# Flamingo block, attention stage: first queries, key stacks, zero rows and a weights' part in another order

## What is computed

```python
x = x + tanh(g_xattn[0]) * attention(layernorm(x), ctx_2048, ctx_2048, gamma)
x = x + tanh(g_ffn[0]) * ffn(layernorm(x), ...)

def attention(q, k, v, gamma):            # 16 x 128 x 512 each, 8 heads
    qk = einsum('bhdq,bhdl->bhql', qh, kh) / sqrt(16)
    return gamma * einsum('bhql,bhdl->bhdq', softmax(qk), vh)

def ffn(x):                               # per token, top 2 of 8 experts
    h = x @ down_w + down_b
    # sum over the two chosen experts e: gate * (gelu(gelu(h) @ w1[e] + b1[e]) @ w2[e] + b2[e])
    # plus 0.1 * the shared expert, then up_w, up_b, and gelu(x) @ core_w + core_b
```

## Time and profile before

| | us |
|---|---|
| median of 3 runs | 739.79 |
| lowest and highest run | 738.60, 742.24 |
| the profiled execution | 746.0 |
| its span | 744.2 |
| first matmul | 15.94 |
| TensorE busy | 688.2 (92%) |
| ScalarE, VectorE, GpSimd busy | 538.1, 532.0, 485.9 |

### The profile page before, as it was taken

One profiled execution on the slowest core, in us unless ns is written; L12 is line 12 of the kernel. 1 busy time (PEld: TensorE's weight loads), 2 busy tenths in 40 slices (PEclk: granted clock), 3 DMA queues, 4 the chain that ended last, 5 costly groups with the idle time before them and its releaser, 6 DMA issues. The chain is left out here.

```text
span 744.2 us, 20867 instructions
## 1 busy us (share of the span) xinstructions
PE 688.2 (92%) x6097; PEld 373.5 (50%) x6097; DVE 532.0 (71%) x853; ACT 538.1 (72%) x1126; POOL 485.9 (65%) x479
## 2 busy tenths in 40 slices
PE   0789999999999999999989998899999999999998
PEld 0122223223333333222354554588888888888744
DVE  4959999999999999999699567634444444444456
ACT  1359999999999999999876647476676767676411
POOL 3555688888888888895577352235666656566632
PEclk9979999999999999999999999999999999999999
DMA  5745565666656765555254552789987888878587
GB/s 161 230 177 162 176 202 158 214 208 199 195 191 201 223 196 188 186 188 174 65 172 152 196 187 90 218 159 167 144 122 115 124 126 112 104 104 97 56 263 261
DMA packets 136289, 123.98 MB, mean 167 GB/s; under 512 B 70548, under 2 KB 105108, under 8 KB 136216
## 3 DMA queue, kind: packets, MB, share of 16 engines
q1 hardware_dynamic: 121352, 106.58, 50.6%
q0 software_dynamic: 13632, 15.47, 14.3%
q10 hardware_dynamic: 1232, 0.98, 0.4%
HBM read 60.33 MB, written 51.53 MB: 150 GB/s over the span
## 5 line engine op out<-in xcount | busy, mean ns | idle before, releaser
L696 DVE TENSOR_REDUCE mx<-nat 128x2 f32<-128x1024 f32 x256 | 298.2, 1213 | 28.3 <-PE nat L527 27.4
L623 ACT ACTIVATE P<-ring 128x512 f32<-128x512 f32 x512 | 277.1, 604 | 21.7 <-PE ring L539 13.7
L2079 POOL DMA_INDIRECT y_sums<-ysb,to x84 | 138.4, 1648 | 99.5 <-DVE ysb L2011 86.4
L552 PE MATMUL pv<-P,VT 128*32 128x256 f32 x2048 | 159.6, 396 | 0.3
L527 PE MATMUL nat<-KS,QS 48*128 48x512 f16 x512 | 110.5, 400 | 29.9 <-DMA QS<-q_scratch 21.6
L539 PE MATMUL ring<-QS,KS 49*128 49x512 f16 x512 | 120.6, 395 | 10.6 <-ACT P L623 8.3
L1622 ACT ACTIVATE X<-EH,bcur 128x256 f32<-128x256 f32 x168 | 85.7, 561 | 51.0 <-DVE u L1975 27.6
L1280 PE MATMUL EH<-XA,whi 128*128 128x256 f16 x672 | 118.4, 275 | 1.9 <-DMA XA<-g_rows 1.9
L1280 PE MATMUL Y<-whi,u 128*128 x672 | 116.9, 273 | 0.3 <-DVE u L1975 0.3
L1975 DVE TENSOR_TENSOR u<-X,u 128x512 f16<-128x512 f32 x84 | 57.8, 688 | 78.9 <-ACT u L1628 78.2
L1280 PE MATMUL EH<-XA,wlo 128*128 128x256 f16 x336 | 92.4, 275 | 0.0
(11 more groups left out here) (264 smaller groups left out, 1003.7 us busy)
## 6 DMA issues: line engine op xcount, KB each, us to landing
XA<-in_wall SPq DMA_DIRECT2D x8, 800.0 KB, 4.6
u<-in_wall SPq DMA_DIRECT2D x8, 800.0 KB, 4.6
QS<-q_scratch SPq DMA_DIRECT2D x64, 96.0 KB, 2.4
KS<-k_scratch SPq DMA_DIRECT2D x62, 96.0 KB, 2.5
X<-in_x SPq DMA_DIRECT2D x16, 256.0 KB, 2.8
q_scratch<-qhl SPq DMA_DIRECT2D x16, 256.0 KB, 2.1
xr<-in_x SPq DMA_DIRECT2D x16, 256.0 KB, 3.9
rd<-den_scratch SPq DMA_DIRECT2D x16, 256.0 KB
```

What stands on the lines that cost most here:

```text
L552: m = pe.matmul(pv[32 * j:32 * j + 32, q], VT[i][:, lb, g, j, :], Pb[4 * (s % 2) + j][:, q], start=(lb == 0 and half == 0), stop=(lb == 3) ...
L623: act.activation(Pb[4 * (s % 2) + j][:, :], bank[:, :], ACT.Exp).then_inc(t_use.sem, 1)
L696: dve.tensor_reduce(mx[:, k // 8, :, k % 8], nat[k % 2][:, :, :], AX.X, ALU.max).then_inc(t_max.sem, 1)
L2079: pool.indirect_dma_start(out=ysum[:, :], out_offset=bass.IndirectOffsetOnAxis(ap=to[:, j % 2, a:a + 1], axis=0), in_=ysb[j % 2][:, a, :], ...
```

## The change

It has five parts. (1) kl of batch 0 moves from GpSimd to VectorE, ahead of qf, and GpSimd's fills wait for ql. (2) In each window the key stacks of both groups are issued right behind the key store, and the query stacks ahead of the u and x1 rows. (3) The weights' part 2 is loaded behind the context in window 1 and not ahead of it. (4) The spare zeros and those of windows 0 to 2 are sent in window 3. (5) The load of context 2 on SyncE and the first key store on ScalarE's queue wait for kl in its new place.

```diff
--- before.py
+++ after.py
@@ -275,7 +275,7 @@
 
     t_cst.plan("all")
     t_lead, t_lead_k = T("dve_lead"), T("act_lead")
-    for what in ("veps", "qf", "qh", "ql"):
+    for what in ("veps", "kl", "qf", "qh", "ql"):
         t_lead.plan(what)
     t_lead_k.plan("kh")
 
@@ -332,7 +332,7 @@
             jobs += [(w - 2, n) for n in ("na", "nb", "num")]
         if w + 1 < B:
             keys, queries = ("kh", "kl"), ("negm", "veps", "rstd", "rs", "qf", "qh", "ql")
-            jobs += [(w + 1, n) for n in (("rstd", "kl") if w < 0 else keys + queries)]
+            jobs += [(w + 1, n) for n in (("rstd",) if w < 0 else keys + queries)]
         if w >= 3:
             jobs += [(w - 3, n) for n in ("xnegm", "xveps", "xrstd", "u", "x1t")]
         if 0 <= w < B:
@@ -408,7 +408,10 @@
             sp.dma_start(xt[b % 2], x[ck.index(b)]).then_inc(t_x[b % 2].sem, 16)
 
         def load_ctx(ck, b):
-            ck.wait(t_pool, b - 2, "kl")
+            if b == 2:
+                sp.wait_ge(t_lead.sem, t_lead.at["kl",])
+            else:
+                ck.wait(t_pool, b - 2, "kl")
             ck.wait(t_ring, b - 2, "vt", 1)
             sp.dma_start(ct[b % 2], ctx_kv[ck.index(b)]).then_inc(t_c[b % 2].sem, 16)
 
@@ -435,7 +438,7 @@
                 for g in range(2):
                     r = DH * (1 - g)
                     sp.dma_start(sd[ck.index(t), 0].rearrange("(j g) q -> g j q", g=2)[g], U[g][r:P:32, :]).then_inc(t_ds.sem, 16)
-            if 1 <= w < B - 1:
+            if 2 <= w < B - 1:
                 load_weights(ck, w + 1)
             if t >= 0:
                 ck.wait(t_ds, t)
@@ -447,6 +450,8 @@
                 sp.dma_start(xr[:, :], x[ck.index(t)]).then_inc(t_xr.sem, 16)
             if 0 <= w < B - 2:
                 load_ctx(ck, w + 2)
+            if w == 1:
+                load_weights(ck, 2)
             if w < 0:
                 sp.wait_ge(t_lead.sem, t_lead.at["ql",])
                 sp.dma_start(sq[0, :, 0:2], qhl[0][:, :, :]).then_inc(t_sq.sem, 16)
@@ -461,6 +466,9 @@
                         sp.dma_start(sd[ck.index(t), 1].rearrange("h (s q) -> (h s) q", s=P // NH), rc[:, :]).then_inc(t_rs.sem, 16)
                     sp.dma_start(scr[ck.index(b), :, 0:2], hl[b % 2][:, :, :]).then_inc(t_.sem, 16)
                     sp.dma_start(scr[ck.index(b), :, 2], hl[b % 2][:, high, :]).then_inc(t_.sem, 16)
+                    if side == 1:
+                        stack(ck, b, 0, 1)
+                        stack(ck, b, 1, 1)
             if b >= B and t >= 0:
                 ck.wait(t_dve, t, "recip")
                 sp.dma_start(sd[ck.index(t), 1].rearrange("h (s q) -> (h s) q", s=P // NH), rc[:, :]).then_inc(t_rs.sem, 16)
@@ -468,28 +476,30 @@
                 ck.wait(t_rs, t)
                 ck.wait(t_pool, t - 1, "att")
                 sp.dma_start(rd[:, :], sd[ck.index(t), 1].unsqueeze(1).broadcast_to([NH, DH, L])).then_inc(t_rb.sem, 16)
+            if 0 <= w and b < B:
+                stack(ck, b, 0, 0)
+                stack(ck, b, 1, 0)
             if s >= 0:
                 ck.wait(t_pool, s, "u")
                 sp.dma_start(us[ck.index(s)], un[:, :]).then_inc(t_us.sem, 16)
                 ck.wait(t_pool, s, "x1t")
                 sp.dma_start(x1s[ck.index(s)], ao[s % 2][:, :]).then_inc(t_st.sem, 16)
                 tail.get((w, "loads"), lambda: None)()
-            if 0 <= w and b < B:
-                stack(ck, b, 0, 1)
-                stack(ck, b, 0, 0)
-            if b < B:
+            if w < 0:
                 stack(ck, b, 1, 1)
                 stack(ck, b, 1, 0)
-            if w < 0:
                 row_of_ones(0)
                 row_of_ones(1)
                 load_weights(ck, 0)
             if w == 0:
                 load_weights(ck, 1)
                 tail["tables"]()
+            if w == 3:
                 sp.wait_ge(t_vt.sem, 4)
                 tail["spare zeros"]()
-            if 0 <= w < B:
+                for n in range(3):
+                    tail["zeros"](ck, n)
+            if 3 <= w < B:
                 tail["zeros"](ck, w)
 
         def last_x1():
@@ -577,7 +587,7 @@
         act.dma_start(ct[0], ctx_kv[0]).then_inc(t_c[0].sem, 16)
         act.wait_ge(t_c[0].sem, t_c[0].at[0,])
         act.copy(khl[0][:, 1, :], ct[0]).then_inc(t_lead_k.sem, 1)
-        act.wait_ge(t_pool.sem, t_pool.at[0, "kl"])
+        act.wait_ge(t_lead.sem, t_lead.at["kl",])
         act.dma_start(sk[0, :, 0:2], khl[0][:, :, :]).then_inc(t_sk.sem, 16)
         act.dma_start(sk[0, :, 2], khl[0][:, 1, :]).then_inc(t_sk.sem, 16)
         act.wait_ge(t_gates.sem, 16 * 3)
@@ -657,6 +667,8 @@
             v, m = ln[0], mv[0]
             dve.wait_ge(t_dve.sem, t_dve.at[0, "aggr"])
             dve.tensor_scalar(v[:, 1:2], m[:, 1:2], EPS, None, ALU.add).then_inc(t_lead.sem, 1)
+            dve.wait_ge(t_lead_k.sem, t_lead_k.at["kh",])
+            dve.tensor_tensor(khl[0][:, 0, :], ct[0], khl[0][:, 1, :], ALU.subtract).then_inc(t_lead.sem, 1)
             dve.wait_ge(t_pool.sem, t_pool.at[0, "rstd"])
             dve.tensor_scalar(qf[:, :], xt[0], m[:, 0:1], v[:, 2:3], ALU.subtract, ALU.mult).then_inc(t_lead.sem, 1)
             dve.wait_ge(t_lead.sem, t_lead.at["qf",])
@@ -779,10 +791,7 @@
                 ck.wait(t_sk, b - 2)
                 done(pool.tensor_scalar(khl[i][:, 1, :], ct[i], 1.0, 1.0, ALU.mult, ALU.mult))
             elif what == "kl":
-                if b == 0:
-                    pool.wait_ge(t_lead_k.sem, t_lead_k.at["kh",])
-                else:
-                    ck.wait(t_pool, b, "kh")
+                ck.wait(t_pool, b, "kh")
                 done(pool.tensor_tensor(khl[i][:, 0, :], ct[i], khl[i][:, 1, :], ALU.subtract))
             elif what == "whi":
                 ck.wait(t_wl[i], b)
@@ -798,6 +807,7 @@
                 if k not in ((B - 1, "att"), (B - 1, "x1")):
                     job(ck, *k)
             if w < 0:
+                pool.wait_ge(t_lead.sem, t_lead.at["ql",])
                 for i in range(2):
                     pool.memset(VT[i][:, :, :, :, :], 1.0).then_inc(t_vt.sem, 1)
                 pool.memset(keep["zs"][:, :], 0.0).then_inc(t_vt.sem, 1)
```

## The result

| | before | after |
|---|---|---|
| median of runs, us | 739.19 (4 runs) | 826.77 (4 runs) |
| lowest to highest | 738.21 to 742.24 | 824.39 to 829.85 |
| ratio | | 1.1171, 95% interval 1.1126 to 1.1217 |
| span of the profiled execution | 744.2 | 828.0 |
| first score | 15.94 | 13.90 |

The change makes the kernel 87.6 us slower; 805 were forecast, 772 to 833 given as range.

The account below looks back on a forecast made before the run. TensorE, VectorE and ScalarE were all taken as nearly full in the attention stage, so common stalls are lost time. -2.3 - 4.9 + 47.6 + 25.2 = +65.6 on the 739.8 median gave 805 us, range 772 to 833.

Parts of the forecast that it names:

- Start: Before the first score: kl on VectorE and later fills free qf from GpSimd's series, gaining 2.3 us.
- Window 1: Zeros and weights leave the queue ahead of the maxima's row; its stall and low clock go, gaining 4.9 us.
- Zero rows later at nothing: Five zero-block issues at the end of window 3 are covered before the next key store, costing nothing.
- the rival "no change": Bundled zero rows make a late maxima's row in window 4 as in window 1: 737.5 us, chance 0.04.
- Stalls: At the starts of windows 2 to 15, group 1's key stack holds SyncE's queue: 3.4 us each, +47.6 us.
- Clock: After each of the 14 stalls TensorE's clock drops: 1.8 us per window, +25.2 us.
- the rival of a steady clock: Stalls at window starts as forecast, but the clock stays up: 780 us, chance 0.16.
- the rival of 931 us: After the stalls the clock never comes back in the windows: 931 us, chance 0.05.
- Sum: Whole kernel: all gains and losses together, +65.6 us.
- The faster rival: At each window's first score, release to query landing under 3.4 us, so no stall: 732.6 us, chance 0.08.

Follow-up runs that it names:

- both_later: The kernel before with only the zero rows and the weights' part 2 sent later: 741.54 us, ratio 0.9999.
- rd_behind: The changed kernel with rd, the broadcast of the reciprocals, issued behind the query stacks: ratio 1.0968 to the kernel before.
- busy_wait: The changed kernel with 24 unused identity products on TensorE ahead of each window's first score: ratio 1.0915 to the kernel before.
- start_alone: The kernel before with only kl of batch 0 on VectorE ahead of qf and GpSimd's fills behind ql: 738.05 us, ratio 0.9965.
- one-line-back kernel: The changed kernel with the key stack of group 1 behind the query stack of group 0 again: 738.92 us, ratio 0.9972.

## Why the prediction was right, and by how much it was off

- **Start**: 2.3 us forecast, 2.04 seen in the changed kernel's trace, 2.5 in the run of its own. GpSimd's whole series had held qf, as read from the row: 3.40 became 0.55. The Trainium skill's rule (SBUF — State Buffer, "SBUF: two separate sides") of one instruction's blocking would have made the step worth 0.6; the run decides against that size. The other half of the rule, that a VectorE operation with two SBUF inputs contends with a GpSimd operation that reads SBUF, fits a small loss in this trace: GpSimd's rstd took 0.95 us beside kl on VectorE (0.57 before).
- **Window 1**: 4.9 us forecast. By the traces it is 5.4: the first score of window 2 comes at 58.90 with 4.40 us of wait, so its place was 54.5, against 61.97 less the start's 2.04.
- **Zero rows later at nothing**: right for the changed kernel, but for a wrong reason, and that is luck. The step named the key store as the next reader behind the five issues and found it covered. The next one that mattered was the denominators' read, 3 us nearer. It comes in time in the changed kernel (the reciprocal at 124.66 does not wait); in the kernel without the stalls it costs 4.0 us by the trace of both_later, and takes back most of what the part before gains. The forecast held the size (4.9, once) in its range and in the rival "no change", by another row than the true one.
- **Stalls**: right in mechanism and place, 14 of them at the starts of windows 2 to 15. Mis-sized: +3.4 us each forecast, of which the trace shows (74.8 - 6.6) / 14 = 4.9, where 6.6 is what windows 2 to 15 waited before, 5.7 for QS and 0.9 for maxima. The steps that failed: from release (190.95) to the second query store 2.5 us, not 2.1; and from the query stack's issue to its score 4.34, not 2.84 to 3.31. The second is the large one. I had taken its duration from places where rd was not queued right ahead, and rd_behind shows that this was it: with rd behind, release to score is 7.28 us (211.61 to 218.89), inside the 7.1 to 7.5 of the prediction. Why the first took 0.4 longer is not tested. These 1.5 us, 14 times, are 21 of the 22 us between forecast and result.
- **Clock**: 1.8 us forecast, 1.9 measured by busy_wait. The clock fell in each stall, the rival of a steady clock is out, and it was up again 4.7 to 6.4 us behind each score, so the rival of 931 us is out too. That 1.8 was so close is in part luck: it was taken from two gaps of other lengths, with bounds of 0 and 2.8.
- **Sum**: -2.0 - 5.4 + 68.2 + 14 x 1.9 = +87.4; the last maxima's record of the stage is 86.9 us later (443.73 against 356.85). The second stage gives back 3.1, so the span is 83.8 us longer. Why it gives back is not tested.
- **The faster rival** fell where its condition said: from release to score are 8.9 us, and it needed less than 3.4.

## What to carry to other kernels

In an in-order issue queue a wait costs what stands behind it, not what it guards: before an item moves forward, ask when its buffer comes free, and who is queued behind. One line (the key stack of group 1 behind the query stack of group 0) separates 12% slower from slightly faster. When transfers are bundled "where there is room", the reader to check is the next small one whose consumer sits inside an engine's busy row, not the next large one. And a duration from issue to use belongs to what was queued ahead of it; take it from a place with the same neighbours.

## What the runs showed of the hardware

- A table of 16 KB, in pieces of 32 bytes from one small source, took 8.0 to 9.5 us to land in thirteen traces, and in 38 to 40 us of the kernel before the DMA engines were 0.05 busy, about one of 16, while x, zeros and weights sent after it had not landed. With it moved, in one execution, weights landed in 7.1 instead of 10.0 us, x in 6.3 instead of 8.7.
- VectorE's qf was held for as long as GpSimd ran instruction after instruction (3.40 us over four of them), not for one.
- TensorE's clock, in the same kernel with the same stalls, stayed at 1.00 once products of no use filled them. An idle 1.14 us (start_alone, 43.20) did not bring it down; the changed kernel's stalls of 4.40 us and more did, all 14.
- The clock's first rise came near 37.6 us in the changed kernel and at about 45 in the one-line-back kernel, which have nearly the same work up to there. Products show it by their lengths (0.61 and 0.38 us for a pair of scores); the profile's clock column does not.
